# A graph-attention kernel on one core: one gather in 64 moved from GpSimd to the sync queue, row by row

## What is computed

```python
def hgt_conv(x, src, dst, ntype, etype, Wk, Wq, Wv, Wa, pri, att, msg, skip):
    k = typed_linear(x, ntype, Wk).reshape(n, H, HD)      # q, v alike
    kw = typed_linear_heads(k[src], etype, att)
    a = jnp.sum(kw * q[dst], axis=-1) * pri[:, etype].T / np.float32(np.sqrt(HD))
    ae = jnp.exp(a - amax[dst])
    w = ae / jax.ops.segment_sum(ae, dst, num_segments=n)[dst]
    m = typed_linear_heads(v[src], etype, msg) * w[:, :, None]
    h = jax.ops.segment_sum(m, dst, num_segments=n).reshape(n, D)
    h = typed_linear(h, ntype, Wa)
    alpha = jax.nn.sigmoid(skip)[ntype][:, None]
    return h * alpha + x * (1.0 - alpha)
```

## Time and profile before

| | us |
|---|---|
| median of 3 runs | 6737.55 (6731.43 to 6742.8) |
| the profiled execution | 6739.41, its span 6737.6 |
| busy: DVE | 5048.9 (75%) |
| busy: PE | 4691.4 (70%) |
| busy: POOL | 4269.9 (63%) |
| busy: ACT | 4031.0 (60%) |

### The profile page before, as it was taken

The page is one execution under the profiler, slowest core; times in us unless marked ns, Lnnn a source line. Parts: engine busy times, 40 slices in busy tenths (PEclk is TensorE's granted clock), DMA queues, the critical chain, the costliest instruction groups (busy, mean ns, idle before and its releaser), DMA issues.

```text
span 6737.6 us, 151874 instructions
## 1 busy us (share of the span) xinstructions
PE 4691.4 (70%) x33354; PEld 4001.1 (59%) x33355; DVE 5048.9 (75%) x14709; ACT 4031.0 (60%) x10574; POOL 4269.9 (63%) x4670
## 2 busy tenths in 40 slices
PE   2976666688666666976666669676666786666664
PEld 1766565566665555765656657665555676555652
DVE  6677777777777777777777777777777778777776
ACT  0466666644766666456666654666666447666661
POOL 0277777724777776267777743777777347777761
PEclk8988878889878887988888779878888898878877
DMA  1633333334333333533333335333333343333331
GB/s 45 255 102 103 104 103 103 103 150 173 101 103 103 104 103 87 211 124 104 103 104 102 103 101 220 102 103 103 104 103 103 141 179 100 103 103 103 103 93 38
DMA packets 273850, 774.98 MB, mean 115 GB/s; under 512 B 88031, under 2 KB 104516, under 8 KB 272708
## 3 DMA queue, kind: packets, MB, share of 16 engines
q0 software_dynamic: 199680, 545.53, 27.5%
q1 hardware_dynamic: 73668, 224.51, 8.6%
HBM read 573.87 MB, written 195.88 MB: 114 GB/s over the span
## 4 chain that ended last, share of the span: by engine, by line
PE 30%; issue 19%; DVEq 19%; DVE 16%; POOL 10%; DMA 4%; ACT 2%; ACTq 1%; POOLq 0%; SPq 0%
POOL rows L462 10%; DVEq L1266 6%; DVEq L1256 5%; PE ps L572 5%; PE ps L749 4%; PE ps L733 4%; PE ps L754 3%; PE ps L596 3%; DMA rows<-table,idx_now 3%; PE ps L583 2%; DVEq L244 2%; PE ps L566 2%; PE ps L748 2%; DVE prod L1250 1%; DVE wmsg L1232 1%
## 5 line engine op out<-in xcount | busy, mean ns | idle before, releaser
L462 POOL DMA_INDIRECT rows<-table,idx_now x4160 | 4036.4, 970 | 1395.6 <-issue 1157.7
L847 ACT ACTIVATE prod<-iota_n,dloc 128x128 bf16<-128x128 f32 x6240 | 1983.5, 389 | 19.6
L748 PE MATMUL ps<-zeros,identb 128*128 128x132 bf16 x2080 | 522.1, 251 | 1543.9 <-DVE wmsg L1232 1267.0
L733 PE MATMUL ps<-qn,ohT 128*128 x8320 | 1444.2, 327 | 76.5 <-issue 56.2
L733 PEld LDWEIGHTS ps<-qn,ohT 128*128 128x128 f32 x8320 | 1266.6, 232 | 154.2 <-issue 135.6
L748 PEld LDWEIGHTS ps<-zeros,identb 128*128 128x128 bf16 x2080 | 227.6, 109 | 1717.3 <-issue 1624.4
L852 ACT ACTIVATE ohf<-prod,ones 128x512 f32<-128x512 bf16 x1040 | 750.7, 722 | 769.8 <-PE ps L754 691.3
L749 PE MATMUL ps<-wmsg,ohf 128*128 128x132 f32 x4160 | 1138.2, 363 | 0.0
L754 PE MATMUL ps<-wmsg,ohf 128*128 128x132 f32 x4160 | 992.0, 328 | 0.0
L1228 DVE TENSOR_TENSOR wmsg<-rows,weight 128x512 f32<-128x512 f32 x1040 | 720.9, 693 | 346.6 <-issue 314.4
L1250 DVE TENSOR_TENSOR prod<-ps,rows 128x512 f32<-128x512 f32 x1040 | 714.8, 687 | 291.1 <-DMA rows<-table,idx_now 162.3
(11 more groups left out here) (166 smaller groups left out, 5516.2 us busy)
## 6 DMA issues: line engine op xcount, KB each, us to landing
table<-rows SPq DMA_DIRECT2D x245, 768.0 KB, 3.3
rows<-table,idx_now POOLq DMA_INDIRECT x4160
rows<-in_node_type SPq DMA_DIRECT2D x5, 2613.0 KB, 10.6
out<-h SPq DMA_DIRECT2D x1, 3072.0 KB
rows<-in_node_type SPq DMA_DIRECT2D x5, 512.0 KB, 4.4
wk<-in_L_gnn_Wk SPq DMA_DIRECT2D x20, 48.0 KB
wq<-in_L_gnn_Wq SPq DMA_DIRECT2D x20, 48.0 KB
wv<-in_L_gnn_Wv SPq DMA_DIRECT2D x20, 48.0 KB
```

Of the source, the lines that this page charges most:

```text
L462: pool.indirect_dma_start(out=rows[:, slot, j, :], out_offset=None, in_=table, in_offset=bass.IndirectOffsetOnAxis(ap=idx_now[:, half, c:c ...
L733: last = pe.matmul(ps[:, 2 + b, j * P:(j + 1) * P], ohT[:, b, j, :], qn[:, at(ts[j]), :].rearrange("p a c -> p (a c)"), start=True, stop=True)
L748: pe.matmul(bank[:, AW:2 * AW], identb[:], zeros[:], start=True, stop=True)
L847: act.activation(squares[:, turn % 2, j * P:(j + 1) * P], iota_n[:], ACT.Square, bias=dloc[:, at(4 * q + j)], scale=-1.0)
```

## The change

The last step of each ring turn (slot 15, j = 3) is no longer gathered by GpSimd, which issues 3 gathers for slot 15 and 4 for the others. SP fetches it. At the start VectorE makes `row_of`: the row numbers of those 13 steps times 1024, as byte offsets. Per turn SP brings one column of it into one partition (`idx_row`), waits, and then eight times loads sixteen offsets into registers and issues sixteen transfers of one row each from a byte view of the table into `stage`. When all eight groups have landed (`s_row`) and slot 15 is free (`s_wm`), one transfer copies `stage` to `rows[:, 15, 3, :]`; VectorE waits for it (`s_side`) as well as for the three gathers. `wa_load` and the next weights are now issued behind all that.

```diff
+            dve.tensor_scalar(row_of[:].rearrange("p (n c) -> p n c", c=1),
+                              idx[:].rearrange("p (n s) -> p n s", s=2 * BS)[:, :, 2 * BS - 1:2 * BS],
+                              float(4 * ROW), None, ALU.mult)
...
+            def index_row(turn):
+                sp.dma_start(idx_row[:], row_of[:, at(turn)]).then_inc(s_irow, 16)
+            def gather_rows(l, turn):
+                hold(sp, s_irow, l * (TURNS * 16) + turn * 16 + 16)
+                for g in range(GROUPS):
+                    _, starts = nc.values_load_multi_w_load_instructions(
+                        idx_row[0:1, g * GROUP:(g + 1) * GROUP], engines=[mybir.EngineType.SP], min_val=0,
...
+                    for j in range(GROUP):
+                        i = g * GROUP + j
+                        sp.dma_start(stage[i:i + 1, :].bitcast(U8), table_bytes[:, at(starts[j], 4 * ROW)]
+                                     ).then_inc(s_row[g], 16)
+            def to_ring(l, turn):
+                for g in range(GROUPS):
+                    hold(sp, s_row[g], l * (TURNS * 16 * GROUP) + turn * (16 * GROUP) + 16 * GROUP)
+                hold(sp, s_wm, l * QUADS + turn * RING + 1)
+                sp.dma_start(rows[:, RING - 1, 3, :], stage[:]).then_inc(s_side, 16)
+            def ring_filled(l, turn):
+                hold(sp, s_side, l * (TURNS * 16) + turn * 16 + 16)
             def edges_(l):
+                index_row(0)
+                gather_rows(l, 0)
+                with sp.Fori(0, TURNS - 1) as turn:
+                    to_ring(l, turn)
+                    index_row(turn + 1)
+                    ring_filled(l, turn)
+                    gather_rows(l, turn + 1)
+                to_ring(l, TURNS - 1)
+                ring_filled(l, TURNS - 1)
                 wa_load(l)
-                hold(sp, s_wa, l * (16 * R4) + 16 * R4)
...
-                    for j in range(4):
+                    for j in range(3 if slot == RING - 1 else 4):
...
-                        dve.wait_ge(s_gath[slot], (l * (QUADS // RING) + use) * 64 + 64)
+                        if slot < RING - 1:
+                            dve.wait_ge(s_gath[slot], (l * (QUADS // RING) + use) * 64 + 64)
+                        else:
+                            dve.wait_ge(s_gath[slot], (l * (QUADS // RING) + use) * 48 + 48)
+                            dve.wait_ge(s_side, (l * (QUADS // RING) + use) * 16 + 16)
```

More of the change, by code:

```diff
@@ L30 @@
 I32 = mybir.dt.int32
+U8 = mybir.dt.uint8
 ALU = mybir.AluOpType
@@ L44 @@
 SP_ = 4 * QUADS
+GROUPS = 8
+GROUP = P // GROUPS
 BS, BQ = 32, 8
 BLOCKS = QUADS // BQ
+TURNS = BLOCKS // 2
 assert BLOCKS * BQ == QUADS and BS * H == P and BS == 4 * BQ
@@ L64, in gnn @@
     table = nc.dram_tensor("table", (TILES * P * ET, ROW), F32, kind="Internal").ap()
+    table_bytes = table.rearrange("(o n) c -> o (n c)", o=1).bitcast(U8)
     table_tiles = table.rearrange("(t p e) c -> t p (e c)", p=P, e=ET)
@@ L88, in gnn @@
         tile_of = sb("tile_of", [1, SP_], I32)
+        row_of = sb("row_of", [P, TURNS], I32)
         idx_now = sb("idx_now", [P, 2, BS], I32)
@@ L124, in gnn @@
         wmsg = sb("wmsg", [P, 2, 4, AW])
+        stage = sb("stage", [P, ROW])
+        idx_row = sb("idx_row", [1, P], I32)
         score = sb("score", [P, 2, P])
@@ L196, in gnn @@
         s_h = sem("h_updated")
+        s_irow = sem("index_row_loaded")
+        s_row = [sem(f"rows_staged{g}") for g in range(GROUPS)]
+        s_side = sem("rows_of_queue_in_ring")
         s_gath = [sem(f"gathered{i}") for i in range(RING)]
@@ L380, in types_load @@
                              ).then_inc(s_types2, 16)
-            def edges_(l):
+            def index_row(turn):
[5 more added lines that the diff above has]
+                        idx_row[0:1, g * GROUP:(g + 1) * GROUP], engines=[mybir.EngineType.SP], min_val=0,
+                        max_val=(TILES * P * ET - 1) * ROW * 4,
+                        skip_runtime_bounds_check_because="an edge's row is 6 times its source node plus its type")
+                    for j in range(GROUP):
[9 more added lines that the diff above has]
+                hold(sp, s_side, l * (TURNS * 16) + turn * 16 + 16)
+            def edges_(l):
+                index_row(0)
[7 more added lines that the diff above has]
+                ring_filled(l, TURNS - 1)
                 wa_load(l)
-                hold(sp, s_wa, l * (16 * R4) + 16 * R4)
                 if not isinstance(l, int):
@@ L388, in edges_ @@
                     hold(sp, s_w, l * WN + 2 * WN)
+                hold(sp, s_wa, l * (16 * R4) + 16 * R4)
             def output_(l):
```

## The result

The changed kernel takes 6665.67 us (median of 5 runs, 6662.1 to 6675.3) against 6737.55 before: 0.9895 of the time, 95% interval 0.9881 to 0.991. That is 71.9 us less; the forecast was 70.

The account below looks back on a forecast made before the run. GpSimd's gathers were taken to bound the edge phases: 12 x 1.27 = 15.3 us per layer less 1, 71 us over five layers, with SP's work hidden. Forecast 6737.55 - 70 = 6668 us, range 6650 to 6790.

Parts of the forecast that it names:

- The bound: Edge phases: GpSimd never rests, each gather costing 1.272 us including a 0.305 us gap, so its gathers set the phase's length.
- The size: Edge phases: twelve gathers fewer give 15.3 us per layer, less 1 us: 14.3 per layer, 71 us in all.
- the step left out: First ring turn of each layer: its removed gather only lengthens the 6.98 us wait at slot 0 and gives nothing.
- the upper bound of 83: All five edge phases: at most 13 x 1.272 x 5 = 83 us can be gained.
- VectorE's reserve: VectorE's waits for gathered rows, 24.5 us in layer 0 to 58.6 in the last, let it follow a faster GpSimd.
- The loss of 1 us for uneven steps: Edge phase, per layer: 1 us taken off because some of VectorE's uneven steps won't line up with GpSimd's pace.
- SP's turn: Sync queue, per ring turn: the new work takes 58 us, ends 47 and 79, hidden under GpSimd's 80.1.
- The forecast gap: SP in each ring turn: 15 to 25 us spent waiting for s_wm, a sign that the forecast is right.
- SP late: Rival, sync queue: row pitch over 0.53 us makes SP outlast GpSimd's turn; 7175 us at 0.60; chance 0.15.
- Landing after landing: Rival, SP's fetches: each row costs a full 2.3 us landing, 306 us a turn, 20,200 us in all; chance 0.03.
- VectorE as the bound: Rival, edge phases: VectorE's turns near 80.9 us leave only 25 to 45 us gain, 6693 to 6713; chance 0.11.
- Slower gathers: Rival, GpSimd: fetches lengthen each gather; by 0.02 us gives 6738 +- 13, chance 0.06; more, up to 6790, chance 0.03.

Follow-up runs that it names:

- the two other parts alone: Changed kernel with all gathers kept, SP's fetches unused, no ring copy: 0.9999 of the kernel before; kernel before with only wa_load and next weights moved later: 1.0001.

## Why the prediction was right

**The bound.** GpSimd's gathers bound the edge phase: plus one, minus one and minus two gathers move the time by +67, -74 and -134 us, and nothing else in the change moves it by an amount that the runs can tell (0.9999 and 1.0001 for the two other parts alone). The reading behind it, that idle time of 0.30 us ahead of each gather is the gather's price and not a reserve, held.

**The size.** 12 x 1.27 = 15.3 per layer less one, 71 us: measured 71.9, and the step left out held too, the wait at slot 0 taking up the first gather. But the agreement of the sum is closer than that of its parts. The edge phases gained 14.0 to 19.9 us each, 84.5, more than the upper bound of 83 allowed, and the phases between lost some of it. In the profile of the kernel with the gather only left out the edge phases gained 69 us and the projection phases stayed as before (178.6 to 179.0 us from the first transfer to the next gather). All three kernels with SP's fetch loop in which SP isn't late had 180.3 to 182.3 in layers 1 to 3, against 178.7 to 179.1 before.

The traces show a cost here that the forecast did not have. SP's program of a layer has grown by the fetch code, and the jump back of the loop over the layers comes just before the edge phase. In the changed kernel the line of that jump reads (`MOVE` is the instruction behind it):

```profile
L304 SPq COMPARE_BRANCH  x1: 45/45/45, 1579.5 to 1579.5; - x1
L304 SPq MOVE  x1: 42/42/42, 1582.1 to 1582.1; - x1
```

And in the kernel before:

```profile
L293 SPq COMPARE_BRANCH  x1: 45/45/45, 1595.6 to 1595.6; - x1
L293 SPq MOVE  x1: 34/34/34, 1595.9 to 1595.9; - x1
```

The jump takes 2.4 to 2.5 us in the changed kernel at layers 1, 2 and 3, and 0.23 before, in the kernel with the gather only left out too. SP is the last engine to arrive there, so GpSimd waits for it and begins 0.97 us after the jump's end in both. First gather of layer 1, before and after:

```profile
1596.90 1.06 POOL L462 DMA_INDIRECT rows<-table,idx_now  x1 [15.40 <-SPq L275]
```

```profile
1583.04 1.06 POOL L510 DMA_INDIRECT rows<-table,idx_now  x1 [17.18 <-SPq L286]
```

That is 3 x 2.2 = 6.6 us of the 8.1 by which these phases grew. So SP's program is hidden inside the edge phases but not at their start, and the forecast put this at nothing. That it came within 2 us of the measured gain all the same is in part luck: in the profile the edge phases gained more than it said. How much more they gain is uncertain: these are single executions, and with all gathers left in place one edge phase of the kernel with unused fetches was 4.9 us shorter than before. The medians can't tell the 6.6 us either.

**VectorE's reserve.** It was read from its waits for rows, and the kernel with four gathers less bore them out roughly: 26.9 against 24.5 us in layer 0, 57.3 against 58.6 in the last, but 31.7 against 23.4 and 34.2 against 25.9 in layers 2 and 3. The loss of 1 us for uneven steps can't be told from the scatter.

**SP's turn.** Forecast 58 us, ends 47 and 79; measured 56.7. The terms missed in both directions and cancelled, which is luck: a row every 0.32 us instead of 0.36 (with the gaps 42 us instead of 46), a load of sixteen registers 1.23 instead of 0.63 (9.9 us instead of 5), near its upper end of four times the load of four; the ring copy 2.6 us from its issue to its landing instead of 3.7; and the loop's end, priced at the 3.2 us of VectorE's jump, only 0.2, with 2.3 us of semaphore instructions and of the index row that were not priced. VectorE's price for a jump is what SP paid as soon as waits or rows were added. The forecast gap of 15 to 25 us per turn was there, at 23.5.

**The rivals.** SP late: not at 0.32 us per row; the two kernels with more rows show its price to be as worked out, a turn for a turn, but for the dearer jump. Landing after landing: excluded for the changed kernel by the kernel that does it. There the priced landing of 2.3 us, read from the weights' burst, was too large. The Trainium skill ("DMA: Bandwidth & Descriptors", section "Anatomy of one DMA — SWDGE (gpsimd) path") fits a fixed 2.0 us per transfer, mostly confirmation of the write. It measured that on GpSimd's queue, and no run here has the same for SP's: a row landed 1.04 us after its issue, well below it, and the ring copy of 128 rows 2.1 us. That the fixed part overlaps was the prediction's conclusion, not the page's; 0.32 us from row to row bears it out. VectorE as the bound: not yet with one gather less; with two the second brings 60 us instead of 74, and with four it is the bound. Slower gathers: 968 ns, no.

## What to carry to other kernels

Where an engine issues without ever being waited for, price a removed instruction at its duration plus the gap that goes with it, and read how much the others can follow from their waits for its results: here those waits (162.3 us) came within 8% of the most that could be had (175.0), though they were not its ceiling. An idle queue can take over such work, even at more than a hundred times the number of instructions, as long as its whole turn stays below the old one. The wait that the view shows at the queue's release was its reserve here (22.6 us of a turn of 79.3). But work put into it can cost more than its own instructions: in the kernels with a longer loop the jump back rose from 0.2 to 2.4 us and more, and at the border of a phase, where the others wait for SP, such a jump holds them up. So look at the loops' ends and at the phases' borders as well, and add work until the time moves.

## What was not expected of the hardware

A gather costs GpSimd nearly the same for 64 rows as for 128 (903 and 946 ns). A transfer of one row with its address from a register holds SP 225 ns, and a load of sixteen registers 1.23 us, four times a row's whole pitch of 0.32. 8320 small transfers beside the gathers did not lengthen these (969 ns against 970). SP's jump back costs either 0.2 us or 2.4 to 3.2 us. Its ring loop has 281 and 284 instructions a turn in the two kernels where the jump takes 0.2 us, and 293 (a wait added to each group), 421, 428 and 557 where it takes 2.4 or more. Eight waits were enough to change it. That the loop's length decides is argued from these six kernels; what SP does in that time is not shown.

On SP's hardware queue the packets rose from 73668 to 109028:

```profile
q1 hardware_dynamic: 109028, 241.62, 9.7%
```

The 35360 more are 65 x 544, and 544 is 2 x 128 for the rows and 2 x (128 + 16) for the ring copy and the index row: two packets per row, read as its data and one completion, where the transfers spread over 16 engines have 16. Two other kernels bear the sum out: without the ring copy there are 9360 = 65 x 144 packets less, and with 64 rows more in a turn 8320 = 65 x 64 x 2 more. That agrees with the Trainium skill (same page, section "Why a DMA increments its semaphore by 16 and not by 1"), by which a transfer with a single outer element runs on one engine.
